# Layer norm of the first attention stage on GpSimd, with its residual rows loaded transposed, one mask less on TensorE and new slot tables for three stages

## The chip, the cores and the metric

The kernel runs on one core of a Trainium2 chip. The metric is the device time of one launch in microseconds (us), lower is better. In the profile TensorE is PE (its weight loads PEld), VectorE DVE, ScalarE ACT, GpSimd POOL and SyncE SP.

## What is computed

The input is `x` of 128 batches x 128 x 256 and a context of the same size. Three attention layers and a feed-forward layer follow each other, each with a residual sum and a layer norm. The change rewrites the end of the first layer and touches the timetables of the second and third:

```python
# first layer; B=128, C=128 channels, L=256 positions, 8 heads of 16
init = q
qh, kh, vh = gconv(q, wq), gconv(k, wk), gconv(v, wv)      # grouped conv, 3 taps
scores = einsum('bhdl,bhdm->bhlm', qh, kh) / sqrt(8)
att = softmax(scores - 1e9 * mask, axis=-1)
o = einsum('bhlm,bhdm->blhd', att, vh).reshape(B, L, C)
x = o + swapaxes(init, 1, 2)                                # residual, transposed
y = (x - mean) * rsqrt(var + 1e-5) * gamma + beta           # over the 128 channels
return swapaxes(y, 1, 2)
# second layer: self-attention, 16 heads, 256 channels, a mask shared by all; out1 = LN(x + attn1)
# third layer: cross-attention to the context, padding mask;   out2 = LN(out1 + attn2)
# feed forward: LN(out2 + relu(out2 @ w1 + b1) @ w2 + b2)
```

## The kernel before

The four layers are four stages with a barrier between them. `attention(phase)` makes stages 0, 1 and 2. Its work is cut into *units* of 512 rows (tokens): 64 units in stage 0 (2 batches of 256 rows each), 32 in stages 1 and 2 (4 batches of 128). A unit has four *tiles* of 128 rows, j = 0 to 3. Names of stage 0 begin with `l_` in the profile, those of stages 1 and 2 with `mha_`.

Work of a unit on the engines, in stage 0:

- **project** (PE, L746): two 128x512 results (`project 0` and `1`, the query and the key side) of nine matmuls each. ACT writes each twice (L916), POOL subtracts (`first_rest`, L1196), ACT rounds (`mid_part`, L983), POOL subtracts again (`low_part`, L1202, which counts `split_done`). The three parts in bf16 are then placed by SP into `l_stack`: `fill_stack` issues ten DMAs for each half of the unit (L678), after `split_done` of both projections.
- **scores** (PE, L783): 16 chunks of two matmuls. DVE adds the mask and takes row maxima from PSUM (`max_of`, L1069). There are two score banks: the scores of chunk i wait until DVE has read chunk i-2. The first chunk waits for the ten DMAs of the first half.
- **max** (POOL L1209 and L1211, PE L792, ACT L931, a DMA on ACT's queue): the maxima of eight chunks are turned and become three more rows of `l_stack`.
- **attend** (PE, L813): 16 chunks of four matmuls, again with two banks. The additive mask comes either from DVE (L1084, one add of 128x512 in PSUM) or, for the chunks listed in `pe_masks`, from two matmuls of 512 columns on PE ahead of the four (L809). ACT takes the exponential (L943).
- **values** (PE L761, ACT L922) and **pv** (PE, L827: 32 small matmuls for a tile). ACT copies the result (`heads_copy`, L948).
- the **finish** of a tile: PE turns the heads (`turn_heads`, L840) and with them the residual rows of the tile (L843), both into one PSUM bank. DVE takes reciprocals (L1102), divides (`merge`, L1109), adds the residual from PSUM (`add`, L1119), computes statistics (L1130, L1134) and adds epsilon (L1139). POOL takes -mean, the power -1/2 and their product (`power`, L1222, L1224, L1227), ACT normalises (`normalise`, L989), POOL multiplies by gamma and adds beta (`affine`, L1236, L1238), PE turns the normalised tile (`turn_y`, L868), and ACT copies that out (L962).

The order on every engine is written by a table, `PLANS[phase]`. A unit is 16 *slots*; attend chunk i stands in slot i. `score` gives the slot of each score chunk, for the unit that comes next (16 and more: in the following body). `steps` and `dve_steps` give the finish of tile j as slot 4j + first number; the second number, 0 to 2, is the place in the slot on DVE (before the scores, between the two halves, after them). `work` lists the uses of the two work banks by slot, the unit they belong to (-1: the one before, 2: two ahead) and the index; a use with two slots is cut into two pieces. Each engine executes its own list in order and meets the others only through semaphores, so a waiting instruction holds back everything behind it on its engine. Within a slot PE runs: attend, pv, scores, work, turns. POOL runs: the max split, `power`, `first_rest`, `low_part`, `affine`, and the rounding rest of a later input (L1183).

Residual rows: `load_resid` (SP, L664) loads the two batches as they lie, channels on partitions. That is why PE must turn them.

```python
steps={'turn': 7, 'normalise': 10},
dve_steps={'recip': (7, 2), 'merge': (7, 2), 'add': (8, 0), 'stats': (8, 1),
           'moments': (9, 0), 'epsilon': (9, 2)},
pe_masks=(1, 4, 6, 9, 12, 13),
```

## Time and profile before

| | |
|---|---|
| median of 3 runs | 4723.11 us (4717.27 to 4725.65) |
| the profiled execution | 4722.3 us |
| its span in the profile | 4720.5 us |
| PE busy | 4284.9 us, 91% of the span |
| DVE busy | 3659.4 us, 78% |
| ACT busy | 3147.0 us, 67% |
| POOL busy | 2939.8 us, 62% |

The stages have different limits, so the shares over the whole span say little about any of them. The profile's page gives each engine's busy time, the span in 40 slices, the costliest groups of instructions by line, and what each engine waited for. The same can be asked for a stretch of time. A name after `<-` in a wait is the instruction that ended it. Matmuls are pipelined: the duration of one includes its way through the array, and the next one starts earlier. What one costs PE is therefore read from the distance between two starts.

### The profile page before, as it was taken

How to read it: one execution, taken by the hardware profiler on the slowest of the kernel's cores; microseconds unless marked ns; L12 is line 12 of the kernel's file. 1: busy time of each engine (PE TensorE's matmuls, PEld its weight loads, DVE VectorE, ACT ScalarE, POOL GpSimd, SP SyncE). 2: the span in 40 equal slices, each digit the busy share in tenths (PEclk: the TensorE clock that was granted, in tenths of full speed). 3: DMA queues.
4: the chain of work that ended last, by engine and by line, in shares of the span. 5: the costliest groups of instructions: out<-in, count | busy, mean ns of one | idle time of the engine just before them, and what ended most of it. 6: DMA issues, size and time to landing. Idle time of an engine off the chain costs nothing. (4 is left out here: it accounts for less than half of the span.)

```text
span 4720.5 us, 151301 instructions
## 1 busy us (share of the span) xinstructions
PE 4284.9 (91%) x46733; PEld 3450.4 (73%) x46733; DVE 3659.4 (78%) x14325; ACT 3147.0 (67%) x6284; POOL 2939.8 (62%) x4394
## 2 busy tenths in 40 slices
PE   5999999999999986898999995899999996999999
PEld 3777777777777755777777774677777875999998
DVE  4888888888888875888888885677787775666665
ACT  3777777777777765777777774577777775444443
POOL 2556565556565645777777774677777773555555
PEclk8999999999999998999999998899999998999999
DMA  4333333333333324555555552666666663222221
GB/s 100 114 111 111 112 110 111 111 111 111 111 111 111 111 75 119 160 156 159 155 162 156 161 150 86 175 190 188 191 193 191 197 181 117 68 67 67 67 80 49
DMA packets 1065927, 602.19 MB, mean 128 GB/s; under 512 B 64664, under 2 KB 1065544, under 8 KB 1065800
## 3 DMA queue, kind: packets, MB, share of 16 engines
q1 hardware_dynamic: 1055816, 595.97, 43.9%
q10 hardware_dynamic: 9984, 4.72, 0.4%
q8 instruction: 56, 0.92, 0.1%
q14 instruction: 71, 0.58, 0.0%
HBM read 175.86 MB, written 117.54 MB: 62 GB/s over the span
## 5 line engine op out<-in xcount | busy, mean ns | idle before, releaser
L1069 DVE CUSTOM_DVE_ANT_0 l_junk<-l_bank,mask 128x256 bf16<-128x256 f32 x2048 | 775.8, 418 | 127.3 <-PE l_bank L783 105.2
L943 ACT ACTIVATE mha_probs<-mha_bank 128x512 f32<-128x512 f32 x1024 | 606.7, 600 | 252.4 <-DVE mha_bank L1084 146.0
L943 ACT ACTIVATE l_probs<-l_bank 128x512 f32<-128x512 f32 x1024 | 611.5, 597 | 234.0 <-DVE l_bank L1084 174.6
L1084 DVE TENSOR_TENSOR l_bank<-l_bank,mask0t 128x512 f32<-128x512 f32 x640 | 445.2, 696 | 101.4 <-PE l_bank L813 90.3
L1069 DVE CUSTOM_DVE_ANT_0 mha_junk<-mha_bank,mask 128x128 bf16<-128x128 f32 x2048 | 466.3, 284 | 67.3 <-PE mha_bank L783 63.8
L813 PE MATMUL mha_bank<-mha_stack 99*128 99x128 bf16 (+1 forms) x4096 | 407.9, 223 | 61.0 <-DMA mha_stack<-mha_max_rows 53.9
L783 PE MATMUL l_bank<-l_stack 96*128 96x256 bf16 x2048 | 369.4, 276 | 70.7 <-DVE l_max_parts L1069 56.6
L783 PE MATMUL mha_bank<-mha_stack 96*128 96x128 bf16 (+1 forms) x4096 | 370.8, 222 | 54.2 <-DMA mha_stack<-mha_parts 37.0
L813 PE MATMUL l_bank<-l_stack 99*128 99x128 bf16 x4096 | 405.8, 221 | 14.7 <-issue 6.5
L1393 ACT ACTIVATE ffn_hidden<-ffn_h,ffn_b_s 128x512 f32<-128x512 f32 x256 | 176.8, 691 | 355.2 <-PE ffn_h L1347 337.3
L813 PEld LDWEIGHTS l_bank<-l_stack 99*128 99x128 bf16 x4096 | 256.5, 99 | 210.1 <-issue 181.2
L1084 DVE TENSOR_TENSOR mha_bank<-mha_bank,mask1t 128x512 f32<-128x512 f32 x512 | 354.6, 693 | 59.0 <-PE mha_bank L813 57.2
L1196 POOL TENSOR_TENSOR mha_yproj<-mha_yproj,mha_parts 128x512 f32<-128x512 f32 x256 | 300.1, 1172 | 160.1 <-ACT mha_parts L916 159.9
L1060 DVE TENSOR_REDUCE mha_max_parts<-mha_bank 128x4 f32<-128x512 f32 x512 | 336.7, 683 | 73.3 <-PE mha_bank L783 70.6
L1360 PEld LDWEIGHTS ffn_o<-ffn_w_parts,ffn_hidden_parts 128*128 128x128 f32 x3072 | 384.9, 191 | 11.6 <-issue 2.0
L1347 PE MATMUL ffn_h<-ffn_x_parts,ffn_w_parts 128*128 128x512 f32 x1536 | 373.8, 393 | 20.6 <-DVE ffn_x_parts L1408 20.6
L1360 PE MATMUL ffn_o<-ffn_w_parts,ffn_hidden_parts 128*128 128x256 f32 x3072 | 388.2, 283 | 1.6 <-DVE ffn_hidden_parts L1413 1.6
L1413 DVE TENSOR_TENSOR ffn_hidden_parts<-ffn_hidden,ffn_hidden_parts 128x512 fp32r<-128x512 f32 x256 | 248.1, 970 | 182.5 <-ACT ffn_hidden_parts L1393 179.5
L813 PEld LDWEIGHTS mha_bank<-mha_stack 99*128 99x128 bf16 (+1 forms) x4096 | 287.1, 99 | 133.7 <-DMA mha_stack<-mha_max_rows 38.0
L783 PEld LDWEIGHTS mha_bank<-mha_stack 96*128 96x128 bf16 (+1 forms) x4096 | 255.3, 99 | 117.8 <-issue 46.7
L1347 PEld LDWEIGHTS ffn_h<-ffn_x_parts,ffn_w_parts 128*128 128x128 f32 x1536 | 282.0, 189 | 74.7 <-issue 21.0
L1202 POOL TENSOR_TENSOR mha_parts<-mha_yproj,mha_parts 128x512 bf16<-128x512 f32 x256 | 297.8, 1163 | 58.8 <-ACT mha_parts L983 56.5
(189 smaller groups left out, 11627.5 us busy)
## 6 DMA issues: line engine op xcount, KB each, us to landing
mha_stack<-mha_parts SPq DMA_DIRECT2D x1536, 128.0 KB, 2.4
l_stack<-l_parts SPq DMA_DIRECT2D x1024, 64.0 KB, 2.0
l_stack<-l_parts SPq DMA_DIRECT2D x256, 128.0 KB, 2.3
cols_o<-mha_y_t SPq DMA_DIRECT2D x128, 256.0 KB, 3.0
l_x_pad<-in_x SPq DMA_DIRECT2D x64, 256.0 KB, 2.7
l_c_pad<-in_ctx SPq DMA_DIRECT2D x64, 256.0 KB, 2.9
l_resid<-in_x SPq DMA_DIRECT2D x64, 256.0 KB, 2.7
...
```

Of the source, the lines that this page charges most:

```text
L783: mm = nc.tensor.matmul(sbank[i % 2][:, s * KEYS:(s + 1) * KEYS], stack[0:SCORED, u.par, place(0, h), j * P:(j + 1) * P], stack[0:SCORED, ...
L813: mm = nc.tensor.matmul(tbank[i % 2][:, s * P:(s + 1) * P], stack[0:STACKED, u.par, place(1, h), key:key + P], stack[0:STACKED, u.par, pla ...
L943: nc.scalar.activation(probs[:, i % RING, :], tbank[i % 2][:, :], ACT.Exp).then_inc(att_exp, 1)
L1060: nc.vector.tensor_reduce(max_parts[:, j, 0, col:col + SH * GROUPS - 1:GROUPS], sbank[i % 2][:, :].rearrange("p (s k) -> p s k", s=SH), op ...
L1069: ins = nc.vector.tensor_tensor_reduce(out=junk[:, i % 2, cols], in0=sbank[i % 2][:, cols], in1=mask, scale=1.0, scalar=LOWEST, op0=ALU.ad ...
L1084: nc.vector.tensor_tensor(bank_, bank_, mask.unsqueeze(1).to_broadcast([P, 4, P]), ALU.add).then_inc(att_masked, 1)
L1196: nc.gpsimd.tensor_tensor(rest, rest, parts[:, u.par, i, HI, :], ALU.subtract).then_inc(rest_step, 1)
L1202: nc.gpsimd.tensor_tensor(parts[:, u.par, i, LO, :], rest, parts[:, u.par, i, MID, :], ALU.subtract).then_inc(split_done, 1)
L1347: mm = nc.tensor.matmul(hbank[f % 4][:, :], w1_parts[:, a, kt, f * P:(f + 1) * P], x_parts[:, u.par, b, kt, :], start=(i == 0), stop=(i == 5))
L1360: mm = nc.tensor.matmul(obank[j][:, 0:L], hidden_parts[:, u.par, b, f, j * P:(j + 1) * P], w2_parts[:, a, f, :], start=(f == 0 and i == 0) ...
L1393: last = nc.scalar.activation(out, hbank[f % 4][:, :], ACT.Relu, bias=c["ffn_b1_s"][:, f:f + 1])
L1413: nc.vector.tensor_tensor(hidden_parts[:, u.par, 1, f, :], hidden[:, f % 2, :], hidden_parts[:, u.par, 0, f, :], ALU.subtract).then_inc(h_ ...
```

## The change

In stage 0:

- The host lays out a transposed copy of `x` beside the others. `load_resid` loads from it, rows on partitions, in the form in which the sum needs them. Its wait is on `z_done` in place of `turn_mm`.
- PE no longer turns the residual (L843 is gone). `turn_heads` waits for `merged_done` in place of `z_done`.
- `merged` has two buffers. The sum of it with the residual is an operation of POOL, from SBUF (`add`), in place of DVE's from PSUM.
- Epsilon is added on POOL, ahead of the power; DVE's epsilon is gone. POOL's -mean and product are gone, because POOL also normalises: one operation with two scalars (subtract mean, multiply by the power). ACT's `normalise` is gone.
- `pe_masks` has five chunks in place of six. DVE adds eleven masks in place of ten.

In stage 1 epsilon moves from DVE to POOL as well, and -mean times the power is one operation after the power. In stage 2 only slots move. All three tables of slots are new.

```diff
     dict(
-        score=[4, 5, 6, 6, 8, 8, 9, 10, 10, 11, 11, 12, 14, 15, 15, 18],
+        score=[4, 4, 5, 6, 7, 8, 9, 10, 11, 12, 12, 13, 14, 15, 15, 18],
         pv_lag=2,
-        steps={'turn': 7, 'normalise': 10},
-        dve_steps={'recip': (7, 2), 'merge': (7, 2), 'add': (8, 0), 'stats': (8, 1), 'moments': (9, 0), 'epsilon': (9, 2)},
-        pe_masks=(1, 4, 6, 9, 12, 13),
+        steps={'turn': 6, 'normalise': 10},
+        dve_steps={'recip': (6, 2), 'merge': (7, 2), 'stats': (9, 1), 'moments': (9, 2)},
+        pe_masks=(1, 4, 6, 13, 14),
         split_lag=0,
+        pool_steps={'add': (7, 0), 'power': (9, 0)},
...
-              ((7, 8), 'project', 2, 0),
-              ((9, 10), 'project', 2, 1),
...
+              ((6, 7), 'project', 2, 0),
+              ((8,), 'turn_y', -1, 2),
+              ((10,), 'project', 2, 1),
+              ((11,), 'turn_y', -1, 3),
...
     dict(
-        score=[4, 4, 5, 7, 7, 8, 9, 10, 11, 12, 13, 15, 15, 16, 16, 19],
+        score=[4, 5, 5, 7, 8, 9, 11, 12, 12, 13, 14, 14, 15, 15, 17, 19],
...
-        steps={'turn': 5, 'turn_merged': 7, 'output': 8, 'normalise': 9},
...
+        steps={'turn': 5, 'turn_merged': 7, 'output': 8, 'normalise': 10},
...
-            res_units = x_units
+            res_units = io["x_t"].rearrange("(u b) (h p) c -> u p (b h) c", b=BU, p=P)
...
-                wait(pe, z_done, n)
-                if conv and j == 0:
-                    pe.wait_ge(resid_ld[u.par], 16 * (u.k + 1))
+                wait(pe, merged_done if conv else z_done, n)
...
-                if conv:
-                    mm = nc.tensor.transpose(fbank[:, 2 * P:3 * P], resid[:, u.par, j * P:(j + 1) * P], c["ident"][:, :])
...
+            def add(u, j):
+
+                n = TILES * u.u + j
+                if j == 0:
+                    pool.wait_ge(resid_ld[u.par], 16 * (u.k + 1))
+                wait(pool, work_mm, turned(u, j, 2))
+                pool.wait_ge(merged_done, n + 1)
+                nc.gpsimd.tensor_tensor(z[:, j % 2, :], merged[:, j % 2, :], resid[:, u.par, j * W:(j + 1) * W],
+                                        ALU.add).then_inc(z_done, 1)
+
             def power(u, j):
                 n = TILES * u.u + j
+                mean, var = moments[:, j % 2, 0:1], moments[:, j % 2, 1:2]
+                r = rstd[:, j % 2, :]
+                if phase != 2:
+                    wait_apart(pool, moments_done, n + 1, passed["pool"])
+                    nc.gpsimd.tensor_scalar(var, var, EPS, None, ALU.add).then_inc(var_done, 1)
+                pool.wait_ge(var_done, n + 1)
+                nc.gpsimd.tensor_tensor(r, var, c["minus_half"][:, :], ALU.pow).then_inc(rstd_done, 1)
+                if phase == 1:
+                    wait_apart(pool, rstd_done, 2 * n + 1, passed["pool"])
+                    nc.gpsimd.tensor_scalar(shift[:, j % 2, :], mean, r, -1.0, ALU.mult, ALU.mult).then_inc(rstd_done, 1)
+
+            def normalise(u, j):
                 r = j % 2
...
+                wait_apart(pool, rstd_done, TILES * u.u + j + 1, passed["pool"])
+                nc.gpsimd.tensor_scalar(z[:, r, :], z[:, r, :], moments[:, r, 0:1], rstd[:, r, 0:1],
+                                        ALU.subtract, ALU.mult).then_inc(normed, 1)
```

The order on POOL in the loop of stage 0, from the subtraction after the second projection to the one that releases the stack's DMAs. `l_yproj` and `l_parts` are the projection and its parts, `l_y` the output row. Before:

```order
L1196 TENSOR_TENSOR l_yproj<-l_yproj,l_parts 128x512
L1236 TENSOR_TENSOR l_y<-l_z,g 128x128
L1238 TENSOR_TENSOR l_y<-l_y,b 128x128
L1201 REGISTER_ALU
L1202 TENSOR_TENSOR l_parts<-l_yproj,l_parts 128x512
```

After:

```order
L1189 TENSOR_TENSOR l_yproj<-l_yproj,l_parts 128x512
L1232 TENSOR_SCALAR l_z<-l_z,l_moments,l_rstd 128x128
L1241 TENSOR_TENSOR l_y<-l_z,g 128x128
L1243 TENSOR_TENSOR l_y<-l_y,b 128x128
L147 REGISTER_ALU
L1212 REGISTER_ALU
L1213 TENSOR_TENSOR l_z<-l_merged,l_resid 128x128
L1194 REGISTER_ALU
L1195 TENSOR_TENSOR l_parts<-l_yproj,l_parts 128x512
```

The normalising of tile 0 and the sum of tile 1 now stand between the two subtractions (L1189 and L1195, before L1196 and L1202).

The order on PE in the same loop, at the turn that stood ahead of attend chunk 12 and its mask. Before:

```order
L840 MATMUL l_bank<-ident,l_heads_out 128x128 x2
L843 MATMUL l_bank<-ident,l_resid 128x128
L144 REGISTER_ALU
L809 MATMUL l_bank<-mask0t_parts,ident_r 128x512 x2
L813 MATMUL l_bank<-l_stack 128x128 x4
L144 REGISTER_ALU
L783 MATMUL l_bank<-l_stack 128x256 x2
```

After, behind the second projection, which is now whole in slot 10:

```order
L746 MATMUL l_bank<-l_c_parts,l_w_parts 128x512 x9
L835 REGISTER_ALU
L838 MATMUL l_bank<-ident,l_heads_out 128x128 x2
L147 REGISTER_ALU
L813 MATMUL l_bank<-l_stack 128x128 x4
L147 REGISTER_ALU
L783 MATMUL l_bank<-l_stack 128x256 x2
```

The residual's turn (L843) is gone, the turn of this tile stands one slot earlier, and chunks 11 and 12 have no mask on PE.

## Rows read from the trace of the kernel before

**Rows 1.** Windows: stages 0, 1, 2; length, busy PE, PEld, DVE, ACT, POOL, clock, DMA
```profile
34.00:1766.00 1732.00, 1626.63 (x19072) 1192.43 (x19072) 1438.76 (x6280) 1197.65 (x2566) 997.73 (x2048) 0.99 0.38 109
1766.00:2918.00 1152.00, 994.89 (x11392) 800.83 (x11392) 952.10 (x5379) 845.75 (x1696) 780.37 (x1088) 0.95 0.52 148
2918.00:3975.00 1057.00, 937.18 (x11648) 795.78 (x11648) 787.75 (x1704) 745.92 (x1476) 765.26 (x832) 0.96 0.62 178
```

**Rows 2.** The same view, the steady 850 us of stage 0
```profile
400.00:1250.00 850.00, 815.27 (x9643) 599.96 (x9641) 724.75 (x3176) 602.89 (x1297) 501.90 (x1033) 1.00 0.38 111
```

**Rows 3.** Waits in those 850 us: in total, times, longest
```profile
PE l_bank L783 <- DVE l_max_parts L1069: 25.1, 64, 0.5
```

**Rows 4.** Groups by line, same 850 us: count | busy us, mean ns | idle before
```profile
L1084 DVE TENSOR_TENSOR l_bank<-l_bank,mask0t 128x512 f32<-128x512 f32 x325 | 226.2, 696 | 49.7 <-PE l_bank L813 44.1 <-issue 3.9
...
L809 PE MATMUL l_bank<-mask0t_parts,ident_r 128*128 128x512 f32 x390 | 136.8, 432 | 0.0
...
L1224 POOL TENSOR_TENSOR l_rstd<-l_moments,minus_half 128x1 f32<-128x1 f32 x129 | 73.7, 571 | 0.0
...
L1119 DVE TENSOR_TENSOR l_z<-l_bank,l_merged 128x128 f32<-128x128 f32 x130 | 37.1, 285 | 8.6
L843 PE MATMUL l_bank<-ident,l_resid 128*128 128x128 f32 x130 | 35.4, 272 | 0.0
...
L1222 POOL TENSOR_SCALAR l_shift<-l_moments 128x1 f32<-128x1 f32 x129 | 29.5, 229 | 140.1 <-DVE l_moments L1139 140.1
...
L1227 POOL TENSOR_TENSOR l_shift<-l_shift,l_rstd 128x1 f32<-128x1 f32 x129 | 24.4, 189 | 10.1
...
L1139 DVE TENSOR_SCALAR l_moments<-l_moments 128x1 f32<-128x1 f32 x129 | 19.5, 151 | 2.2
```

**Rows 5.** Timeline of PE, 897.5 to 907 us: start, length, what
```profile
899.84 0.27 PE L843 MATMUL l_bank<-ident,l_resid 128*128 128x128 f32 x1
899.87 0.71 PE L809 MATMUL l_bank<-mask0t_parts,ident_r 128*128 128x512 f32 x2
900.43 0.40 PE L813 MATMUL l_bank<-l_stack 99*128 99x128 bf16 x4
900.66 0.38 PE L783 MATMUL l_bank<-l_stack 96*128 96x256 bf16 x2
...
905.52 0.27 PE L843 MATMUL l_bank<-ident,l_resid 128*128 128x128 f32 x1
905.62 0.39 PE L813 MATMUL l_bank<-l_stack 99*128 99x128 bf16 x4
```

**Rows 6.** Timeline of all engines, 885 to 892 us, from a unit's second projection
```profile
885.10 1.67 PE L746 MATMUL l_bank<-l_c_parts,l_w_parts 128*128 128x512 f32 x6
...
887.97 1.16 POOL L1196 TENSOR_TENSOR l_yproj<-l_yproj,l_parts 128x512 f32<-128x512 f32 x1 [0.20 <-ACT l_parts L916]
...
889.09 0.45 POOL L1236 TENSOR_TENSOR l_y<-l_z,g 128x128 f32<-128x128 f32 x1
...
889.27 0.29 DVE L1109 TENSOR_TENSOR l_merged<-l_bank,l_recips 128x128 f32<-128x128 f32 x1
...
890.03 1.16 POOL L1202 TENSOR_TENSOR l_parts<-l_yproj,l_parts 128x512 bf16<-128x512 f32 x1
```

**Rows 7.** Timeline of SP's queue, 880 to 945 us
```profile
891.29 13.15 SPq L678 DMA_DIRECT2D l_stack<-l_parts  x20
```

**Rows 8.** DMA issues of the page: KB each, us to landing
```profile
l_stack<-l_parts SPq DMA_DIRECT2D x1024, 64.0 KB, 2.0
```

**Rows 9.** Line L1069 on DVE: duration min/median/max in ns, first and last start
```profile
L1069 DVE CUSTOM_DVE_ANT_0 l_junk<-l_bank,mask x2048: 404/419/426, 62.0 to 1742.4; 128x256 bf16<-128x256 f32 x187
```

**Rows 10.** The same for line L1095, the normalising of stage 2
```profile
L1095 DVE TENSOR_SCALAR mha_z<-mha_z,mha_moments,mha_rstd x128: 402/414/1366, 2998.0 to 3967.6; 128x256 f32<-128x256 f32 x128
```

**Rows 11.** Waits in 900 us of stage 1: in total, times, longest
```profile
PE mha_bank L813 <- DMA mha_stack<-mha_max_rows: 40.4, 27, 1.5
```

**Rows 12.** Waits in 700 us of stage 2
```profile
PE mha_bank L868 <- DVE mha_z L1095: 34.4, 23, 1.5
```

92 lines of the change are left out of this document (37 added, 55 removed).

## The prediction

> **What bounds the kernel now.** First the windows by stage [rows 1]. Stage 0 takes 1732 of 4720.5 us and is where nearly the whole change lies. PE is busy for 94% of it, and for 815.27 of 850 us, 96%, once the loop is steady [rows 2], at a granted clock of 1.00. DVE follows with 724.75, 85%; ACT has 71%, POOL 59%. So PE is the bound, and DVE is close behind it. Next the waits: of PE's 35 us without work in that stretch, 25.1 are score matmuls that waited for DVE's row maxima [rows 3]. PE and DVE hold each other: two score banks, and DVE must have read one before PE fills it again.
>
> The length of a unit comes from a count: the residual's turn runs four times in a unit and 130 times in 850 us [rows 4], so there are 32.5 units, 26.2 us each. 64 such units are 1677 us, the rest of the stage is filling and draining. Per unit PE is busy 25.1 us, DVE 22.3, POOL 15.4.
>
> **The change part by part, stage 0.** *PE.* A chunk's mask on PE occupies it from the start of L809 to the start of the four matmuls behind it: 899.87 to 900.43, 0.56 us [rows 5]. One of six goes: -0.56. A residual's turn costs 0.10 where attend follows (905.52 to 905.62) and 0.03 where a mask follows (899.84 to 899.87), since the mask's own weight load is then exposed anyway [rows 5]. The mask's 0.56 holds in both places, so four turns cost between 4 x 0.03 = 0.12 and 4 x 0.10 = 0.40. Half of them stand ahead of a mask in the old order: 0.26. The durations of 272 ns [rows 4] are mostly way through the array and are not saved. PE: -0.56 - 0.26 = **-0.8 us** for a unit, bounds -0.7 and -1.0.
>
> *DVE.* Four sums of 285 ns and four epsilons of 151 ns go, 1.74 us; one mask of 696 ns comes [rows 4]: **-1.05 us**. The sum also waited for the merge just ahead of it: 8.6 us of idle time before 130 sums [rows 4], 0.26 us a unit, goes too.
>
> *ACT* loses four normalisings and is not the bound. *POOL* loses -mean and the product, 4 x (229 + 189 ns) [rows 4], and gets three operations for each tile. Epsilon: 229 ns as the same form. The sum, two inputs of 128x128: 450 ns, as L1236 [rows 6]. The normalising, one input of 128x128 with two scalars, has no row. Its ends are a one-column operation (229 ns) and the two-input one (450); I take 370, nearer to the upper since it carries as many elements. Net 4 x (229 + 450 + 370 - 418) = +2.5 us: POOL goes from 15.4 to 17.9 us of 25. It has room, so its length is free; its order isn't.
>
> The Trainium skill ("GPSIMD Engine Reference", Engine selection) says to leave elementwise sums to VectorE, GpSimd being about two times slower with two inputs. The rows show 450 against 285 ns, 1.6 times, so the direction agrees. By that rule alone the move costs 4 x 165 ns of engine time; by the rows that time falls on an engine with 10 us to spare.
>
> *POOL's order.* What SP's DMAs for the next stack wait for is the last subtraction (L1202). Its way now: the second projection ends on PE at 885.10 + 1.67 = 886.8; ACT; L1196 from 887.97 to 889.13; L1202 from 890.03; SP starts at 891.29 [rows 6, 7]. That is 4.5 us. Between the two subtractions stood only the affine pair. Now a normalising and a sum stand there as well: +0.37 + 0.45 = +0.8 us, with queue distances +0.9. The sum also waits for DVE's merge of tile 1. That ends at 889.56 [rows 6], and POOL would reach the sum at about 890.5, so it is covered by 0.9 us. Queued behind a late one are this subtraction, SP's 20 DMAs and the scores of the next unit. Twenty issues take 13.15 us, 0.66 each [rows 7], landing takes 2.0 [rows 8]: the tenth lands 9 x 0.66 + 2.0 = 7.9 us after the first issue, at 899.2. PE's first score that needs it starts at 900.66 [rows 5]: slack 1.5 us. Of it 0.9 is used up; 0.6 remains, and it is smaller still where PE gets there earlier. So I cut the unit in two. From the projection's end to that score PE now takes 13.9 us; by the order its work there is the same within 0.2 (three residual turns less, a score and a `turn_y` more, three turns and four masks in both). The DMA way is 4.5 + 0.9 + 7.9 = 13.3 us. This part becomes 13.3 to 14.0. The other part, 12.3 us, loses a mask, a score, a `turn_y` and a residual turn, about 0.9 us: 11.3 to 11.5. Together **24.6 to 25.5, middle 25.1**.
>
> *Check with the shares.* PE is busy 25.1 us of 26.2 and would be busy 24.3, DVE 21.3 of 25.1. If the 1.1 us without work stays, the unit is 25.4; if it shrinks with DVE's load by a quarter, 25.15. I take **25.2**, a gain of 1.0 us for a unit, 64 x 1.0 = **-64 us**. Bounds 24.6 and 25.5: -102 and -45.
>
> The residual load's new wait (all sums of the unit two before) is older than the store ahead of it in SP's queue, which needs that unit finished: nothing. Its rows are 512 bytes in place of 1 KB, one DMA of 21 or so in a unit: nothing. `turn_heads` waits for the merge in place of the later sum, and a second `merged` buffer goes with it: nothing or a small gain.
>
> **Stages 1 and 2.** Stage 1: POOL has the same number of operations (229 + 571 + about 229 in place of 229 + 571 + 189 ns), DVE sheds 4 x 151 ns. PE there waits 1.5 us, 27 times in 900 us, so about once in each of 32 units of 1152 / 32 = 36 us, for the row maxima at the first attend chunk [rows 11]. The new table puts four scores in place of two between the turn of those maxima and that chunk, useful work in a wait: -0.5 us. But the last score of that half moves from slot 10 to 12, one ahead of the turn, which may now wait for DVE: +0.5. Both ends for 32 units: -16 to +16. Stage 2: PE waits 1.5 us a unit for the normalising at the second `turn_y` [rows 12], which is itself stretched (median 414 ns, longest 1366 [rows 10]). Its slot moves one back while `turn_y` stays; between the wait gone for two thirds and half as long again: -32 to +24. I take **-6** for both together.
>
> **Sum.** 4722.3 (span 4720.5 and 1.8 around it) - 64 - 6 = **4652 us**. The profiled execution lies 0.8 below the median of 4723.11; the prediction is rounded over that.
>
> **The rivals.** *A: the wait only moves* (gain 0.4 us a unit). The second projection is now nine matmuls in a row in slot 10 with nothing for DVE in between; if DVE runs dry there, it is late in the slots with two scores. Against it: DVE has 3.8 us of a unit free. 0.4 x 64 = 26: **4694**. Chance 0.17.
>
> *B: slower, through the stack.* If POOL reaches the last subtraction 2 us later than I reckon (normalising nearer 450, and the sum kept back by a DVE that lags more than 0.9 us, every unit), the first part is 15.3 us, the unit 15.3 + 11.4 = 26.7: +0.5 x 64 = +32, **4748** with stages 1 and 2 at -6. It decides from 1.5 us on, where 14.8 + 11.4 is the old 26.2. For it: 0.6 us of slack in the profile. Against: the merge is early by 0.9. Chance 0.10.
>
> *C: DVE is blocked by POOL's added work.* In stage 2 the normalising, all in SBUF, ran 1366 ns where its median is 414 [rows 10]: it lay beside a POOL subtraction. If stage 0's maxima suffered the same, four times (450 + 370 ns) = 3.3 us, DVE would need 24.6 us and the unit would stay at 26.2: **4716**. Against it, L1069 runs 404 to 426 ns over the whole stage, beside POOL's 59% [rows 9], and the change leaves DVE no operation in stage 0 with two tensors in SBUF. The Trainium skill ("SBUF — State Buffer", on the shared port pair) says that DVE and GpSimd exclude each other for a whole instruction where DVE has two SBUF inputs or a two-port mode. Both rows agree with that. Chance, with every other way to no change: 0.09.
>
> *D: more than the sum.* Part one at 13.3 and part two at 11.3, and the wait of stage 1 filled: -102 - 16: **4604**. Chance 0.14.
>
> My forecast, 4625 to 4680: 0.50.
>
> **How the numbers follow.** About 0.2%, 9.4 us, is what a measurement of this kernel can tell from no change. Faster is my forecast, D and A: 0.81. Same: 0.09, of it C most. Slower: B, 0.10. The range for 8 in 10 holds forecast and A and takes in the bounds of stages 1 and 2 and most of D: **4603 to 4714**; outside lie B, most of C and the far end of D, 0.2 together.
>
> **What would show it.** Right: the count of a once-a-unit line gives a unit of 25.2 us; PE still at 95% or more and no L843; DVE near 21.3 us of a unit; the normalising on POOL 300 to 450 ns; SP's 20 DMAs starting 5.4 us after the end of the second projection, not 4.5; stages 1 and 2 within 20 us of 1152 and 1057. Wrong: a wait of PE's scores for the stack's DMAs in every unit (B); DVE idle behind the long projection, PE idle in the slots after it (A); L1069 with a long maximum (C); a granted clock under 1.00 in the steady stretch of stage 0, where it now has none; or stages 1 and 2 moving by more than stage 0.

## The result, and the profile after

| | changed kernel | before |
|---|---|---|
| median | 4781.57 us (4 runs, 4776.62 to 4786.02) | 4722.99 us (4 runs, 4717.27 to 4725.65) |
| ratio | 1.0125, 95% interval 1.0108 to 1.0143 | 1 |
| span of the profiled execution | 4784.2 us | 4720.5 us |

The change makes the kernel **58.6 us slower**, 1.2%. Forecast were 4652 us, with 4603 to 4714 as the range. The measured time lies 130 us above the one and 68 above the other.

First the windows by stage: stretch, its length, and the busy time of PE, PEld, DVE, ACT and POOL, then the granted clock and the DMA share. The stages are cut here at the first load that SP issues for each, in both kernels (34.0, 1773.7, 2919.2 and 3978.5 before), since the bounds of [rows 1] were round numbers. Cut so, the lengths before are 1739.7, 1145.5 and 1059.3 us, with the same busy times as in [rows 1]. Lengths in the text are from bounds to 0.01 us, so they can differ by 0.1 from a row whose bounds are rounded (stage 2 below is 1092.8).

```profile
34.20:1801.80 1767.60, 1588.99 (x18688) 1193.72 (x18688) 1370.49 (x5832) 1082.91 (x2310) 1276.75 (x2304) 0.96 0.37 107
1801.80:2949.10 1147.30, 1013.28 (x11392) 799.09 (x11392) 948.41 (x5251) 846.05 (x1696) 790.44 (x1088) 0.95 0.52 148
2949.10:4042.00 1092.90, 942.59 (x11648) 797.16 (x11648) 774.72 (x1704) 751.32 (x1476) 756.64 (x832) 0.95 0.60 172
```

Stage 0 is 27.9 us longer than before, stage 2 is 33.5 us longer, and stage 1 is the same within 2 us. The feed-forward stage is unchanged (742.2 against 742.0). In stage 0 PE executes 384 matmuls fewer than before (18688 against 19072), and is busy for 37.6 us less (1626.63 - 1588.99). Its time without work, length minus busy, grew from 113.1 to 178.6 us. The clock fell as well, from 0.98 to 0.96. So the work taken from PE did leave it. More waiting came in than work went out.

The steady stretch of stage 0 is next, in the same view (answers to [rows 2]), and then the waits of PE in it (answers to [rows 3]).

```profile
400.00:1250.00 850.00, 782.68 (x9346) 589.05 (x9344) 681.88 (x2913) 538.15 (x1153) 637.99 (x1153) 0.98 0.38 110
```

```profile
PE l_bank L864 <- POOL l_z L1232: 33.3, 32, 1.0
PE l_bank L783 <- DVE l_max_parts L1065: 22.1, 32, 0.7
```

The second row was there before, with nearly the same length (25.1). The first is new: once in every unit `turn_y`, now L864, waits for the normalising on POOL, L1232. The unit is 26.6 us (the merge runs 128 times in 850 us, so 32 units), where it had been 26.2 and was to be 25.2.

The groups by line in that stretch, on POOL (count | busy us, mean ns | idle before and its releaser), answer to the prices taken from [rows 4] and [rows 6]:

```profile
L1232 POOL TENSOR_SCALAR l_z<-l_z,l_moments,l_rstd 128x128 f32<-128x128 f32 x129 | 105.5, 818 | 13.5 <-POOL l_rstd L1224 13.5
...
L1224 POOL TENSOR_TENSOR l_rstd<-l_moments,minus_half 128x1 f32<-128x1 f32 x128 | 72.9, 570 | 10.7
...
L1213 POOL TENSOR_TENSOR l_z<-l_merged,l_resid 128x128 f32<-128x128 f32 x128 | 58.6, 458 | 0.2
...
L1222 POOL TENSOR_SCALAR l_moments<-l_moments 128x1 f32<-128x1 f32 x128 | 29.1, 228 | 80.6 <-DVE l_moments L1127 80.6
```

The sum took 458 ns (450 forecast) and epsilon 228 (229). The normalising took **818 ns**, against 370 forecast and an upper bound of 450.

One place in the timeline shows the whole wait (start, length, engine, what, idle time before it and releaser):

```profile
906.34 0.18 DVE L1127 BATCH_NORM_AGGREGATE l_moments<-l_stats 128x2 f32<-128x6 f32 x1
...
906.72 0.23 POOL L1222 TENSOR_SCALAR l_moments<-l_moments 128x1 f32<-128x1 f32 x1 [0.33 <-DVE l_moments L1127]
...
906.96 0.78 PE L783 MATMUL l_bank<-l_stack 96*128 96x256 bf16 x4
907.03 0.57 POOL L1224 TENSOR_TENSOR l_rstd<-l_moments,minus_half 128x1 f32<-128x1 f32 x1
...
907.81 0.82 POOL L1232 TENSOR_SCALAR l_z<-l_z,l_moments,l_rstd 128x128 f32<-128x128 f32 x1 [0.21 <-POOL l_rstd L1224]
...
908.78 0.30 PE L864 MATMUL l_bank<-ident,l_z 128*128 128x128 f32 x1 [1.04 <-POOL l_z L1232]
```

PE has finished its scores at 907.74. The moments were ready at 906.52. From there the three operations and the distances between them take until 908.63, 2.11 us in all. They stand in a row, each needs the one before, and the second `turn_y` stands in slot 15, right behind them: PE stands from 907.74 to 908.78.

### The profile page after: what moved, and what is told of

Its sections match the earlier page's. It is cut to its first block and busy times, and to the rows that moved or that the text cites. A ratio compares the mean times of both kernels' runs of the same rounds, so it can differ in the third digit from the quotient of the medians.

```text
span 4784.2 us, 150223 instructions
## 1 busy us (share of the span) xinstructions
PE 4271.4 (89%) x46349; PEld 3451.0 (72%) x46349; DVE 3575.8 (75%) x13749; ACT 3038.0 (64%) x6028; POOL 3220.9 (67%) x4650
## 5 line engine op out<-in xcount | busy, mean ns | idle before, releaser
L1065 DVE CUSTOM_DVE_ANT_0 l_junk<-l_bank,mask 128x256 bf16<-128x256 f32 x2048 | 779.2, 418 | 114.0 <-PE l_bank L783 102.6
L1080 DVE TENSOR_TENSOR l_bank<-l_bank,mask0t 128x512 f32<-128x512 f32 x704 | 487.7, 693 | 201.1 <-PE l_bank L813 198.8
L1065 DVE CUSTOM_DVE_ANT_0 mha_junk<-mha_bank,mask 128x128 bf16<-128x128 f32 x2048 | 467.8, 284 | 64.0 <-PE mha_bank L783 60.4
L783 PE MATMUL mha_bank<-mha_stack 96*128 96x128 bf16 (+1 forms) x4096 | 385.4, 223 | 119.9 <-DVE mha_max_parts L1065 43.8
L783 PE MATMUL l_bank<-l_stack 96*128 96x256 bf16 x2048 | 386.5, 275 | 59.2 <-DVE l_max_parts L1065 48.6
L813 PE MATMUL l_bank<-l_stack 99*128 99x128 bf16 x4096 | 409.1, 223 | 17.4 <-issue 12.4
L1189 POOL TENSOR_TENSOR mha_yproj<-mha_yproj,mha_parts 128x512 f32<-128x512 f32 x256 | 297.3, 1161 | 171.5 <-ACT mha_parts L912 169.8
L813 PE MATMUL mha_bank<-mha_stack 99*128 99x128 bf16 (+1 forms) x4096 | 403.2, 223 | 7.7 <-DMA mha_stack<-mha_max_rows 3.3
L813 PEld LDWEIGHTS l_bank<-l_stack 99*128 99x128 bf16 x4096 | 271.6, 99 | 169.6 <-issue 133.3
L1195 POOL TENSOR_TENSOR mha_parts<-mha_yproj,mha_parts 128x512 bf16<-128x512 f32 x256 | 298.0, 1164 | 96.0 <-ACT mha_parts L979 72.8
L813 PEld LDWEIGHTS mha_bank<-mha_stack 99*128 99x128 bf16 (+1 forms) x4096 | 289.1, 99 | 79.4 <-issue 25.9
```

What stands on the lines that cost most here:

```text
L783: mm = nc.tensor.matmul(sbank[i % 2][:, s * KEYS:(s + 1) * KEYS], stack[0:SCORED, u.par, place(0, h), j * P:(j + 1) * P], stack[0:SCORED, ...
L813: mm = nc.tensor.matmul(tbank[i % 2][:, s * P:(s + 1) * P], stack[0:STACKED, u.par, place(1, h), key:key + P], stack[0:STACKED, u.par, pla ...
L1065: ins = nc.vector.tensor_tensor_reduce(out=junk[:, i % 2, cols], in0=sbank[i % 2][:, cols], in1=mask, scale=1.0, scalar=LOWEST, op0=ALU.ad ...
L1080: nc.vector.tensor_tensor(bank_, bank_, mask.unsqueeze(1).to_broadcast([P, 4, P]), ALU.add).then_inc(att_masked, 1)
L1189: nc.gpsimd.tensor_tensor(rest, rest, parts[:, u.par, i, HI, :], ALU.subtract).then_inc(rest_step, 1)
L1195: nc.gpsimd.tensor_tensor(parts[:, u.par, i, LO, :], rest, parts[:, u.par, i, MID, :], ALU.subtract).then_inc(split_done, 1)
```

## The experiments

**Theory T, the chain** (called C in the last two runs): what is lost in stage 0 is the wait of the second `turn_y` for moments, epsilon, power and normalising; POOL's load as such costs nothing. **Rivals:** the slots chosen are bad as a whole (R), or the work on POOL costs by its amount (R3 and Q: it delays the stack's DMAs, or POOL is too full), or the size of the one operation is all of it (S). Every run is one kernel with its own profile. The ratio is against the kernel before, run on the same chip. Stage lengths are from each kernel's own windows, cut as above. All these kernels compute everything, except the last two, which say what they leave out.

### e1: normalising back on ACT, in the new slots

```diff
-                    if phase == 1:
+                    if phase != 2:
                         for at in finish_in(t, slot, "normalise"):
                             normalise(*at)
...
-                if phase == 1:
+                if phase != 2:
                     wait_apart(pool, rstd_done, 2 * n + 1, passed["pool"])
                     nc.gpsimd.tensor_scalar(shift[:, j % 2, :], mean, r, -1.0, ALU.mult, ALU.mult).then_inc(rstd_done, 1)
...
-        score=[4, 5, 6, 7, 7, 8, 9, 9, 11, 12, 14, 14, 14, 16, 17, 19],
+        score=[4, 5, 6, 7, 7, 8, 9, 9, 11, 12, 13, 14, 15, 16, 17, 19],
```

> Stage 0: the changed kernel with the normalising back on ACT (POOL computes -mean times the power, as in stage 1); sum, epsilon, mask count and slots stay as changed. Theory T (the chain moments, epsilon, power, 818 ns normalising on POOL is too long for the second turn_y of a unit, PE waits 1.04 us there): the chain gets about 0.2 us for the product and 0.49 us for ACT in place of 0.82, so the wait shrinks to 0.6 to 0.9 us, and POOL sheds 4 x 0.8 us: stage 0 falls from 1768 us by 15 to 40 us. Rival R (the loss comes from the slots: two scores in slot 12, the long projection in slot 10, not from POOL): stage 0 stays within 5 us of 1768. Stage 2, a second edit of its own: the three score chunks in slot 14 are spread to 13, 14 and 15. If PE's 1.24 us wait for DVE's maxima there is what was added, stage 2 falls from 1093 by 25 to 40 us; if only the wait for the normalising counts, by less than 10. Stage 1 is untouched.

Measured: 4798.19 us, ratio 1.0155 (1.0138 to 1.0171). Stage 0 took 1802.6 us, 35 more than in the changed kernel. Its clock was 0.98, and PE was busy for only 1570.89 us (1588.99 there), so the 35 us and 18 more are waiting. That fits neither theory: T had 15 to 40 us less, R no change. The waits of PE in 400 to 1250 us, and one of ACT's:

```profile
PE l_bank L838 <- ACT l_heads_out L944: 25.0, 31, 0.8
PE l_bank L783 <- DVE l_max_parts L1065: 22.2, 32, 0.7
PE l_bank L792 <- ACT l_parts L912: 20.9, 32, 0.7
PE l_bank L864 <- ACT l_z L985: 13.0, 31, 0.4
PE l_bank L813 <- ACT l_probs L939: 11.3, 31, 0.4
```

```profile
ACT l_z L985 <- POOL l_shift L1227: 99.3, 88, 1.5
```

The wait at `turn_y` fell from 33.3 to 13.0. In its place the rest of ACT's queue is late: ACT's normalising waits for POOL's product, 99.3 us in 850, and holds what stands behind it (PE's three waits for ACT at L838, L792 and L813 are new or far longer). So taking the dear operation off POOL and giving it to ACT doesn't help in these slots. Stage 2 with the three scores apart took 1072.2 us, against 1092.8.

### e2: the second turn_y into slot 1 of the next body

```diff
         work=[((0,), 'values', 1, 0),
+              ((1,), 'turn_y', -1, 1),
...
               ((13,), 'turn_y', 0, 0),
-              ((15,), 'turn_y', 0, 1)],
# stage 2: 'normalise': 10 -> 9
```

> Stage 0: the changed kernel with the second turn_y of a unit moved from slot 15 to slot 1 of the next body; POOL still normalises. Theory T (only the place where PE meets the late tile costs): the 1.04 us wait goes and stage 0 falls from 1768 to about 1700 (64 units x 1.0 to 1.26 us). Rival R (slots and DVE): the wait turns up at the next score or attend and stage 0 falls by less than 15 us. Stage 2, an edit of its own: normalise stands in slot 4j+9 again, all else as changed. If the wait for the normalising (1.35 and 0.9 us a unit) is what was added, stage 2 falls from 1093 by 25 us or more; if the three scores in slot 14 are, by less than 10. Stage 1 is untouched.

Measured: 4786.53 us, 1.0138 (1.0121 to 1.0154), the sum of a large gain and a large loss. **Stage 0 fell from 1767.6 to 1669.8 us.** PE there is busy for 1551.72 us, with the same 18688 matmuls that had taken 1588.99, at a clock of 0.99:

```profile
34.20:1704.00 1669.80, 1551.72 (x18688) 1160.21 (x18688) 1370.65 (x5832) 1073.01 (x2310) 1272.79 (x2304) 0.99 0.39 113
```

That is 30 us below the 1700 that theory T expected. POOL's work is the same as in the changed kernel (1272.79 against 1276.75). So this amount of it isn't what costs; where PE asks for the result is. Stage 2 rose to 1194.7 us. One slot earlier, the normalising meets POOL's power in the same slot, DVE stands for it, and the maxima queue up behind. The waits in 3100 to 3850 us:

```profile
PE mha_bank L783 <- DVE mha_max_parts L1056: 49.8, 21, 2.8
...
DVE mha_z L1091 <- POOL mha_rstd L1224: 44.3, 43, 1.6
```

### e3: the old tables for stages 1 and 2

The changed kernel with the tables of before in stages 1 and 2. Its operations stay: stage 1 still adds epsilon on POOL.

```diff
# stage 2, core of it
-        score=[4, 5, 6, 7, 7, 8, 9, 9, 11, 12, 14, 14, 14, 16, 17, 19],
-        steps={'turn': 5, 'turn_merged': 7, 'output': 8, 'normalise': 10},
-        split_lag=1, pool_steps={'power': (9, 2)}, split_slot=14,
+        score=[4, 5, 7, 7, 8, 9, 9, 10, 11, 12, 12, 14, 16, 16, 18, 19],
+        steps={'turn': 5, 'turn_merged': 7, 'output': 8, 'normalise': 9},
+        split_lag=0, pool_steps={'power': (8, 1)}, split_slot=13,
```

> The changed kernel with the tables of stages 1 and 2 of the kernel before (epsilon of stage 1 stays on POOL). Both theories: stage 0 stays at 1768, stage 2 returns to 1059 within 3 us, so the whole falls by about 33 us to 4749. Stage 1 tells what epsilon on POOL costs by itself: 1145 if nothing, 1155 or more if POOL's extra 40 ns and DVE's relief matter there.

Measured: 4760.3 us, 1.0077 (1.006 to 1.0094). Stage 0 stays at 1768.4. Stage 2 is back at 1063.7 us (1059.3 before), so the loss of stage 2 is its new table. Stage 1 took 1157.6 us. That is the one value of the old table with epsilon on POOL; the new table gave 1134.8 to 1147.8 in the thirteen kernels that have it. The new table of stage 1 thus earns some 10 to 23 us, and the move of epsilon costs about 12 (1157.6 against 1145.5), each read from one profile.

### e4: the normalising as two operations

```diff
-                nc.gpsimd.tensor_scalar(z[:, r, :], z[:, r, :], moments[:, r, 0:1], rstd[:, r, 0:1],
-                                        ALU.subtract, ALU.mult).then_inc(normed, 1)
+                nc.gpsimd.tensor_scalar(z[:, r, :], z[:, r, :], moments[:, r, 0:1], None,
+                                        ALU.subtract).then_inc(centred, 1)
+                wait_apart(pool, centred, TILES * u.u + j + 1, passed["pool"])
+                nc.gpsimd.tensor_scalar(z[:, r, :], z[:, r, :], rstd[:, r, 0:1], None,
+                                        ALU.mult).then_inc(normed, 1)
```

Stage 2 has both edits of e1 and e2.

> Stage 0: the changed kernel with POOL's normalising made of two operations with one scalar each in place of one with two, a wait between them. It lengthens the chain: theory T expects each 0.1 us more in the two together (with their gap) to show as 0.1 us more for a unit, 6.4 us for the stage. If the two take 2 x 0.45 us and a gap of 0.1, stage 0 gets 10 to 15 us longer; if each costs 0.8 us, 50 us. If one scalar costs less than half of 0.8 us, it gets faster. Rival R expects less than 5 us either way. Stage 2: both edits of the two runs before together (scores spread, normalise in 4j+9): with both waits gone it is at or under the 1059 us of the kernel before.

Measured: 4925.72 us, 1.0427 (1.041 to 1.0445). Stage 0 rose to 1852.0 us, 84 more. The two operations took 620 and 607 ns in the median, with 0.2 us between them: the chain is 1.43 - 0.82 = 0.61 us longer, 64 x 0.61 = 39 us. The wait in 400 to 1250 us grew to 1.8 us a time:

```profile
PE l_bank L865 <- POOL l_z L1236: 53.1, 30, 1.8
```

So the direction of theory T is right, but each us of chain costs two of the stage. Of the 84 us, 57 are time without work and 27 are PE's own work, which took longer at a clock of 0.95 (1616.26 us busy). Stage 2 took 1154.1 us: the scores apart don't undo the harm of the earlier normalising.

### e5: the late turn_y with the old table of stage 2

The edit of e2 in stage 0, the new table of stage 1, and the old table of stage 2 as in e3.

> The changed kernel with the second turn_y of stage 0 moved to slot 1 of the next body (stage 0 took 1669.8 us so) and the old table for stage 2 (1063.7 us so). Theory T (stage 0's gain was eaten by the wait at that turn_y, stage 2's loss is its table): 34.5 + 1670 + 1137 to 1147 + 1061 to 1064 + 742 = 4645 to 4658 us, 1.4% under the kernel before. If the two stages are not independent, more.

Measured: **4647.17 us** (5 runs, 4642.79 to 4652.61), ratio 0.9842 (0.9829 to 0.9856). It beats both kernels, and it is the prediction's 4652 within 5 us. The agreement is in part chance: stage 0 gained 70.5 us and not 64, and stages 1 and 2 together changed by +0.6 and not by -6, with the table of stage 2 taken back. Its stages, and its waits of PE in 400 to 1250 us:

```profile
34.30:1703.50 1669.20, 1551.47 (x18688) 1160.00 (x18688) 1370.77 (x5832) 1072.56 (x2310) 1272.72 (x2304) 0.99 0.39 113
1703.50:2847.30 1143.80, 1012.51 (x11392) 799.33 (x11392) 948.42 (x5251) 846.07 (x1697) 788.81 (x1088) 0.94 0.52 149
2847.30:3908.90 1061.60, 935.47 (x11648) 794.27 (x11648) 788.29 (x1704) 745.72 (x1476) 765.64 (x832) 0.96 0.61 177
```

```profile
PE l_bank L783 <- DVE l_max_parts L1065: 23.5, 34, 0.7
PE l_bank L813 <- DMA l_stack<-l_max_rows: 5.8, 21, 0.4
```

### e6: e5 with six masks on PE

```diff
-        pe_masks=(1, 4, 6, 13, 14),
+        pe_masks=(1, 4, 6, 9, 13, 14),
```

> The kernel of the run before with attend chunk 9 masked on PE again (six chunks). It prices the mask: if PE bounds every slot, stage 0 gets 0.56 us x 64 = 36 us longer (1706); if DVE's 0.70 us less in slot 9 helps as much, 0 to 10 us; if DVE bounds that part of the unit, it gets shorter. Stages 1 and 2 as the run before.

Measured: 4679.63 us, 0.9918 (0.9903 to 0.9933). Stage 0 is 35.8 us longer (1705.0 against 1669.2), 0.56 us for each of 64 units. That is the mask's price in the prediction to the second digit, and it says that PE is still the bound. By the medians it is 32.5 us.

### e7: e5 with the normalising as two operations

The edit is that of e4, in e5.

> The kernel of the first run of this call with POOL's normalising in two operations (620 and 607 ns against 818): 0.5 us more in the chain with the gap, 1.6 us more of POOL for a unit. With turn_y in slot 15 this cost stage 0 84 us. Theory T: the chain now ends in slot 1, some 3 us later, so this costs under 10 us. Rival R3 (POOL's load delays the subtraction that SP's stack DMAs wait for): 30 us or more, since that order has not changed.

Measured: 4738.31 us, 1.0034 (1.0022 to 1.0046). Stage 0 rose by 86.9 us to 1756.1, and no `turn_y` waits. Theory T in its strict form, POOL's length is free once that turn is late, falls here. Rival R3 had the size, 30 us or more, but not the way: no score waits for the stack in this stretch. The wait is elsewhere, in 400 to 1250 us:

```profile
PE l_bank L814 <- ACT l_probs L940: 27.2, 32, 1.1
```

The timeline of ACT and POOL before one of these waits shows how POOL gets to it (L1170 are two small copies that fill the edges of a later unit's input, `pad_edges`; L975 is ACT's rounding of that input):

```profile
902.94 0.61 POOL L1236 TENSOR_SCALAR l_z<-l_z,l_rstd 128x128 f32<-128x128 f32 x1 [0.20 <-POOL l_z L1233]
903.64 0.46 POOL L1245 TENSOR_TENSOR l_y<-l_z,g 128x128 f32<-128x128 f32 x1
904.18 0.46 POOL L1247 TENSOR_TENSOR l_y<-l_y,b 128x128 f32<-128x128 f32 x1
...
904.70 0.19 POOL L1170 COPY l_c_pad<-l_c_pad 128x4 f32<-128x4 f32 x1
```

```profile
904.93 0.63 ACT L975 ACTIVATE l_x_parts<-l_x_pad 128x516 fp32r<-128x516 f32 x1 [2.11 <-POOL l_c_pad L1170]
905.47 0.62 ACT L975 ACTIVATE l_c_parts<-l_c_pad 128x516 fp32r<-128x516 f32 x1
905.99 0.58 ACT L940 ACTIVATE l_probs<-l_bank 128x512 f32<-128x512 f32 x1
```

The two copies (the second is shown) take 0.19 us each. They need nothing of this tile and stand in POOL's queue behind its normalising and affine. ACT stood 2.11 us for them, and the exponentials that PE wants for its next product were behind that.

### e8: before with only the late turn_y, and only the new scores

```diff
# the kernel before; stage 0
+              ((1,), 'turn_y', -1, 1),
-              ((15,), 'turn_y', 0, 1)],
# stage 2, old table
-        score=[4, 5, 7, 7, 8, 9, 9, 10, 11, 12, 12, 14, 16, 16, 18, 19],
+        score=[4, 5, 6, 7, 7, 8, 9, 9, 11, 12, 14, 14, 14, 16, 17, 19],
```

> The kernel before with two edits. Stage 0: its second turn_y in slot 1 of the next body. There PE waited only 0.25 us at it, so theory T expects 1740 to fall by 5 to 25 us at most: the move gives little without the operations that were moved off PE and DVE. If the move alone brings 50 us or more, the moved operations were worth nothing. Stage 2: the old table with only the new score slots (three in slot 14): if the scores are what costs, 1059 becomes 1080 or more; if it is the later normalise, split and max, it stays within 8 us.

Measured: 4856.75 us, 1.0289 (1.0273 to 1.0304). Stage 0 took 1730.3 us, only 9.4 less than before. The late turn is worth little where the normalising is on ACT. So the 98 us of e2 are not a gain that lay in the old kernel too. Stage 2 took 1204.1 us, 145 more: PE waits 94.5 us in 750 for the maxima.

### e9: the new operations in the old slots

```diff
# stage 0: the changed operations, with before's numbers
-        steps={'turn': 6, 'normalise': 10},
-        pe_masks=(1, 4, 6, 13, 14),
-        pool_steps={'add': (7, 0), 'power': (9, 0)},
+        steps={'turn': 7, 'normalise': 10},
+        pe_masks=(1, 4, 6, 9, 12, 13),
+        pool_steps={'add': (8, 0), 'power': (9, 2)},
# and its score, dve_steps, work and split_slot; stage 2: the new table with the old score
```

> Stage 0: the changed operations (transposed load, sum, epsilon and normalising on GpSimd) in the slots and with the six masks of before: sum in 4j+8, power in 4j+9, second turn_y in slot 15. Theory T (the chain moments, epsilon, power, normalising of 818 ns is too long for the slot of the second turn_y): TensorE waits about 1 us a unit for it here as well, and stage 0 is 1740 us or longer. Rival R (the new slots are what is bad, not the operations): 1700 or shorter. Stage 2: the new table with the old score slots: 1070 us or less if the three scores in one slot are its cost, 1085 or more if not. Stage 1 as in the changed kernel.

Measured: 5085.99 us, 1.0773 (1.0754 to 1.0792), far worse than either theory had meant. Stage 0 took 2017.0 us, at a clock of 0.88. That lies in theory T's "1740 us or longer", but not for its reason, since the wait it names is the small one. The waits in 400 to 1250 us:

```profile
DVE l_stats L1123 <- POOL l_z L1213: 133.9, 83, 2.6
...
PE l_bank L783 <- DVE l_max_parts L1065: 75.9, 111, 1.0
...
PE l_bank L864 <- POOL l_z L1232: 8.9, 28, 0.4
```

In the old slots DVE's statistics stand for a sum that POOL hasn't done yet, 1.6 us each time, with the row maxima behind them. So with these operations the old slots are far worse than the new ones, of which one number alone had to change (e5). That every other new number is needed isn't shown. Stage 2 took 1154.6 us with the new table and the old scores, so the three scores in one slot are not its cost by themselves. Either half of that table without the other is worse than the whole.

### e10: e7 with the two small copies first

They move one slot forward, ahead of that slot's epsilon and power.

```diff
+                    if conv and slot == SPLIT_SLOT - 2 and exists(t.plus(3), N):
+                        pad_edges(t.plus(3))
                     for pos in range(3):
                         ...   # epsilon and power
...
-                    if conv and slot == SPLIT_SLOT - 1 and exists(t.plus(3), N):
-                        pad_edges(t.plus(3))
```

> The kernel with the second turn_y in slot 1, the old table of stage 2 and the normalising as two one-scalar operations, and one edit more: the two small copies into the padded buffers (L1170) stand on GpSimd ahead of the epsilon and power of their slot, not behind the normalising and affine of the tile. Theory P (the 87 us of the two operations come through GpSimd's queue: the normalising holds the two copies, these hold ScalarE's rounding at L975, which waited 2.11 us for them, and that holds the exponentials of the next unit, for which TensorE waits 0.8 to 1.3 us): the wait of TensorE for L940 ahead of the first attend goes, the unit falls from 26.5 to 25.5 us or less, the median from 4738 to 4690 or less. Rival Q (GpSimd is simply too full, at 688 of 850 us, or it holds VectorE through shared access to SBUF): the unit stays at 26.2 or more, the median within 20 us of 4738.

Measured: 4679.77 us, 0.9915 (0.9898 to 0.9931), 58.5 less than e7. Stage 0 fell from 1756.1 to 1705.4, and the wait of L814 for the exponentials is gone. Theory P, the way through the copies, is confirmed for 51 of the 87 us, and rival Q (POOL simply too full, a median within 20 us of e7) falls. 36 are left against e5. Half of those are PE's busy time (1569.52 against 1551.47, at a clock of 0.98 instead of 0.99), half are waits (135.9 against 117.7 us). Among these is, for the first time, one for the stack (the same stretch, PE's waits):

```profile
PE l_bank L784 <- DMA l_stack<-l_parts: 4.6, 16, 0.5
```

### e11: e5 with the two small copies first

The edit is that of e10, in e5.

> The same move of the two small copies in the kernel with the second turn_y in slot 1, the old table of stage 2 and the normalising as one operation. Theory P: ScalarE's rounding starts up to 1.3 us earlier, the 0.28 us a unit that TensorE waits for the exponentials ahead of the first attend goes, 64 times: 4647 to about 4630. Rival Q: within 8 us of 4647, since the copies had been in time, or slower, since epsilon and power start 0.3 us later.

Measured: 4645.28 us (4642.12 to 4649.03), 0.9843 (0.9827 to 0.9859). Stage 0 was 6 us shorter in its profile (1663.1), the median 1.9 below e5. By the median that is no difference, and theory P's 4630 is missed: the copies were nearly in time in e5.

### e12: e5 with the normalising on DVE

```diff
-        steps={'turn': 6, 'normalise': 10},
+        steps={'turn': 6, 'normalise': 11},
...
-                    if phase == 2:
+                    if phase != 1:
                         for at in finish_in(t, slot, "normalise"):
                             normalise(*at)
...
-                        if conv:
-                            normalise(*at)
                         affine(*at)
```

The middle part is in DVE's list (its line there is L1091), the last in POOL's.

> The kernel with the second turn_y in slot 1 and the old table of stage 2, the normalising of stage 0 on VectorE at the end of the slot after the power, not on GpSimd. If what matters of the normalising is only its length in GpSimd's queue: that queue loses 0.82 us a tile, VectorE gains under 0.2 us a tile, and the kernel takes 4647 or less (down to 4630). If VectorE's queue is the tighter one (TensorE waits 19.5 us in 430 us for its maxima already): the wait for the maxima grows by up to 0.2 us a tile, 4647 to 4700.

Measured: 4648.87 us, 0.9852 (0.9836 to 0.9868), the same as e5. In stage 0 POOL is busy 213 us less (1059.66 against 1272.72) and DVE 68 us more, and neither matters: with the turn late, both engines have room. It also says that, with the turn late, the 0.82 us on POOL cost nothing.

```profile
L1091 DVE TENSOR_SCALAR l_z<-l_z,l_moments,l_rstd x135: 335/339/539, 403.6 to 1247.8; 128x128 f32<-128x128 f32 x135
```

### e13 and e14: the changed kernel with a shorter normalising

Still open was which step had failed, the size of the operation or the chain. Both kernels are the changed one with its own slots.

```diff
-                nc.gpsimd.tensor_scalar(z[:, r, :], z[:, r, :], moments[:, r, 0:1], rstd[:, r, 0:1],
+                nc.gpsimd.tensor_tensor(z[:, r, :], z[:, r, :], rstd[:, r, :].to_broadcast([P, W]),
-                                        ALU.subtract, ALU.mult).then_inc(normed, 1)
+                                        ALU.mult).then_inc(normed, 1)
```

```diff
-                nc.gpsimd.tensor_scalar(z[:, r, :], z[:, r, :], moments[:, r, 0:1], rstd[:, r, 0:1],
+                nc.gpsimd.tensor_scalar(z[:, r, 0:1], z[:, r, 0:1], moments[:, r, 0:1], rstd[:, r, 0:1],
                                         ALU.subtract, ALU.mult).then_inc(normed, 1)
```

e13, the first, leaves the subtraction of the mean out. e14, the second, leaves out 127 of the 128 columns.

> The changed kernel; its normalising on GpSimd does only the product with the reciprocal deviation, as one operation on two tensors of 128x128 (a form that takes about 456 ns), and leaves the subtraction of the mean out. The chain ahead of the second turn_y is 0.36 us shorter. Theory S (the size of the operation was the fault): the wait of 1.26 us a unit for it goes, with what stands behind, and stage 0 falls from 1768 to 1700 us or less. Theory C (the chain itself was the fault, whatever the size within the bounds predicted): the wait falls by 0.36 us to about 0.9, stage 0 by 64 x 0.36 = 23 us to about 1745, and the median to about 4758.

> The changed kernel; its normalising on GpSimd treats one column of 128 alone (about 230 ns) and leaves the other 127 out. The chain is 0.59 us shorter than in the changed kernel and at the lower bound of what was predicted for the operation. Theory S: stage 0 at 1700 us or less. Theory C: a wait of about 0.67 us a unit is left, stage 0 about 1768 - 64 x 0.59 = 1730, the median about 4744.

Measured: 4710.42 us, 0.9985 (0.9973 to 0.9996), and 4711.29 us, 0.9984 (0.9974 to 0.9994), 10 runs each. The line's duration (min/median/max ns), first e13, then e14, and e13's stage 0:

```profile
L1232 POOL TENSOR_TENSOR l_z<-l_z,l_rstd x133: 397/400/403, 401.3 to 1246.4; 128x128 f32<-128x128 f32 x133
```

```profile
L1232 POOL TENSOR_SCALAR l_z<-l_z,l_moments,l_rstd x133: 379/382/392, 400.5 to 1246.3; 128x1 f32<-128x1 f32 x133
```

```profile
34.30:1733.70 1699.40, 1548.50 (x18688) 1161.40 (x18688) 1369.09 (x5832) 1083.23 (x2310) 1165.63 (x2304) 0.99 0.38 111
```

The operations came out at 400 and 382 ns, not at 456 and 230, so the two runs are one point twice. By luck it is close to the 370 that the prediction took. Stage 0 is 1699.4 us (1698.6 in e14). That is a hair inside theory S's bound of 1700, and far below the 1745 and 1730 of theory C. It is also 30 us above the 1669.2 that the same stage takes with the late turn, and in 400 to 1250 us `turn_y` still waits:

```profile
PE l_bank L864 <- POOL l_z L1232: 18.9, 33, 0.6
```

Both were at fault, and the next section puts a size to each.

## Why the prediction was wrong

**Stage 0, by its three parts.** With the turn late, stage 0 is 1669.2 us, 70.5 below the old 1739.7. So -64 was a good sum for everything that it counted; up to 9 of the 70 us can be the late turn's own (e8). From there to the changed kernel's 1767.6 are 98.4 us, and e13 cuts them in two:

| stage 0 | length | PE busy | PE without work | clock |
|---|---|---|---|---|
| before | 1739.7 | 1626.6 | 113.1 | 0.98 |
| e5, turn late | 1669.2 | 1551.5 | 117.7 | 0.99 |
| e13, op of 400 ns, turn in slot 15 | 1699.4 | 1548.5 | 150.9 | 0.99 |
| changed kernel, op of 818 ns | 1767.6 | 1589.0 | 178.6 | 0.96 |

- **The step left out: 30 us.** The prediction listed POOL's order only for what SP waits for. It said of POOL's added work "so its length is free; its order isn't", and then priced one order. The other consumer, the second `turn_y`, was never held against its chain: PE's wait there stood in the sum at nothing. From e5 to e13 the time without work grows by 33.2 us, 0.5 us a unit. With an operation of 400 ns, near its own 370, stage 0 gains 40 us (e13) and not the 64 forecast.
- **The term mis-sized: 68 us.** 818 ns instead of 370, above the upper bound of 450. The bounds came from a one-column operation and from one with two inputs. Neither is the form with two scalars on 128 columns. From e13 to the changed kernel the time without work grows by 27.7 us. That is the operation itself: 64 x (818 - 400 ns) = 26.8 us. The rest, 40.5 us, is PE's own work taking longer: the same 18688 matmuls in 1589.0 instead of 1548.5 us. These 68 us need both faults: with the turn late, a normalising of 0.82 us on POOL and one of 0.34 us on DVE give the same stage (1669.2 in e5, 1668.2 in e12).
- **Those 40 us go with the clock.** The steady stretch had a granted clock of 1.00 before [rows 2] and has 0.98 now. What stands ahead of one fall, in the windows of the changed kernel:

```profile
930.00:936.00 6.00, 4.41 (x60) 2.90 (x51) 4.75 (x26) 3.38 (x9) 5.12 (x12) 1.00 0.55 155
936.00:940.00 4.00, 4.00 (x44) 3.24 (x47) 0.82 (x3) 1.48 (x3) 3.06 (x5) 0.57 0.36 98
```

```profile
934.61 0.30 PE L864 MATMUL l_bank<-ident,l_z 128*128 128x128 f32 x1 [1.04 <-POOL l_z L1232]
935.31 0.39 PE L813 MATMUL l_bank<-l_stack 99*128 99x128 bf16 x4 [0.40 <-issue]
```

PE stood for 1.04 us at `turn_y` and 0.40 behind it, and was busy for 4.41 of 6 us. Then it worked without a gap at 1.2 GHz instead of 2.4 for most of 4 us. In windows of 2 us the clock of the changed kernel is under 0.99 at ten places between 400 and 1250 us, a stretch with 32 such waits; in e5, where `turn_y` doesn't wait, and in e13, where it waits 0.6 us, at no place. So the longer wait came with a second price here. What brings the clock down is not shown, though. No run held the wait and changed the clock alone, and the sum of the waits doesn't decide it: e7 lost more of the same stretch to them (72.8 us against 67.3), with single waits of up to 1.1 us at L814, and its clock stayed at 1.00.

```profile
400.00:1250.00 850.00, 777.18 (x9389) 576.97 (x9388) 686.15 (x2917) 531.55 (x1154) 687.73 (x1286) 1.00 0.38 110
```

The prediction had named "a granted clock under 1.00 in the steady stretch" as a sign that it was wrong, and gave it no price.

**PE's terms were right, if small.** The mask's 0.56 us was confirmed by e6 (35.8 / 64). In the stretch at clock 1.00, PE was busy for 815.27 us in 32.5 units before, 25.1 us each, and in e5 for 811.89 us in 33.75 (135 merges), 24.1: -1.0, the far bound of -0.8. The unit of e5 is 25.2 us, as forecast. DVE at 21.3 us a unit (681.88 / 32) was right too.

**The stack (rival B) was read with more care than it was worth.** POOL's last subtraction now starts at 905.23 and SP at 906.48, 5.96 us after the projection's end at 900.52 (forecast 5.4; the operation's extra 0.45 makes the difference). No wait of PE's scores for it shows among the waits of the steady stretch. e10, with an operation more in that queue, shows its first signs, 0.5 us at most. Rival B had the right sign, but not the cause; its 4748 us is still 34 below what was measured. The slack of 1.5 us, of which the prediction left 0.6, was therefore not what gave way.

**Rival A**, PE waiting for DVE behind the long projection, didn't come either: PE's waits for the maxima are 22.1 us where they were 25.1 [rows 3], and e5 has the unit of 25.2. (By its own terms, 4722.3 - 26 - 6, its time is 4690, not 4694; nothing hangs on that.) **Rival C** didn't come: the maxima, L1065, run 404 to 427 ns over the whole stage (before: [rows 9]).

**One input or two on POOL.** e12's normalising took 339 ns on DVE, and the changed kernel's 818 on POOL: 2.4 times. The Trainium skill ("GPSIMD Engine Reference", Engine selection) gives a factor of about two for two inputs and calls one input "roughly line-rate". The first was used in the prediction and agreed in direction (1.6 times). By the second the one-input operation would have been the cheaper one. Here, with two scalars, it is the dearest elementwise operation of its size on POOL (818 against 458 ns for two inputs), so for this form the measurement decides against it.

**Stage 1** is 1.8 us longer, within -16 to +16. Both halves were there: by e3 about -10 for the table and about +12 for epsilon on POOL, read from single profiles, where kernels with the same table spread over 13 us.

**Stage 2: +33.5 us, outside the -32 to +24.** The prediction looked at one edit of that table, the slot of the normalising against `turn_y`. That wait grew no longer (before: [rows 12]). Waits of PE in 750 us of stage 2 of the changed kernel:

```profile
PE mha_bank L864 <- DVE mha_z L1091: 36.2, 38, 1.2
PE mha_bank L783 <- DVE mha_max_parts L1056: 25.7, 24, 1.1
```

The second row has no counterpart before. It comes once a unit, 1.07 us, and 32 units make 34 us, as much as the whole loss. It is a score that waits for DVE, in slot 14, where the new table has three scores for two banks. But setting them apart gave back 20.6 us (e1) and left most of this wait (22.7 us), now in slot 15. So the match of 34 and 33.5 doesn't show that this wait is the loss, and three scores in one slot are not its only reason. In the timelines of both kernels DVE works through the finish of a tile (L1118 to L1132) and a cast (L1086, 0.8 us) ahead of the maxima that the score waits for; no run changed that alone. That the table as a whole is the cause is shown: every kernel with the old one has 1055.4 to 1063.7 us, those with the new one 1092.3 to 1093.7. Why neither half of it works without the other (1204.1 and 1154.6) stays open.
